# Finding the rows of each expert: one-hot tables for two experts, scattered records for six

## The reference

```python
logits = xf @ gate_w.T                      # xf: rotated rows, 4096 x 512; 8 experts
scores = softmax(logits); topv, topi = top_k(scores, 2)
gates = topv / sum(topv)
# loc: running number of a token at its expert, first choices of all tokens first
valid = loc < cap                            # cap = 1024
flat_idx = where(valid, topi * cap + loc, 0)
# per expert: h = relu(rows @ fc1.T + b1); eo = h @ fc2 + b2   (hidden width 2048)
out = x + sum_k eo[flat_idx_k] * gates_k * valid_k
```

## Time and profile before

| | us |
|---|---|
| median of three runs | 1426.5 |
| the profiled execution | 1426.91 |
| its span, first to last instruction | 1425.2 |
| TensorE busy in the span | 1370.5 |
| VectorE busy | 1062.8 |
| ScalarE busy | 702.3 |
| GpSimd busy | 303.1 |

### The profile page before, as it was taken

How to read it: one execution, slowest core, us unless ns; L and a number is a source line. 1 busy time by engine, 2 the same in 40 slices (tenths; PEclk the granted TensorE clock), 3 DMA queues, 4 the chain that set the end, 5 groups by cost and what they waited for, 6 DMA issues and landing times.

```text
span 1425.2 us, 17919 instructions
## 1 busy us (share of the span) xinstructions
PE 1370.5 (96%) x6109; PEld 1123.8 (79%) x6109; DVE 1062.8 (75%) x1610; ACT 702.3 (49%) x1050; POOL 303.1 (21%) x322
## 2 busy tenths in 40 slices
PE   8459999999999999999999999999999999999997
PEld 5347888888888888888888888888888888888885
DVE  6898879686886778686886878777796868855443
ACT  5336445555464455454465445554455454644442
POOL 1054302321024202231033201241032200220021
PEclk9759999999999999999999999999999999999999
DMA  8666575556466564575566564575555533543232
GB/s 296 230 164 143 119 157 146 174 121 148 83 197 157 115 129 129 145 163 132 97 176 167 105 139 108 163 168 135 98 169 145 112 79 61 161 119 68 51 105 71
DMA packets 448684, 194.15 MB, mean 136 GB/s; under 512 B 398432, under 2 KB 400617, under 8 KB 446674
## 3 DMA queue, kind: packets, MB, share of 16 engines
q1 hardware_dynamic: 426466, 125.98, 40.0%
q0 software_dynamic: 22128, 67.03, 14.9%
HBM read 153.21 MB, written 39.98 MB: 136 GB/s over the span
## 4 chain that ended last, share of the span: by engine, by line
PE 94%; DVE 3%; DMA 1%; issue 1%; ACT 0%; SPq 0%; POOL 0%; POOLq 0%; DVEq 0%
PE ps L1163 15%; PE ps L1155 15%; PE ps L1159 15%; PE ps L1130 14%; PE ps L1132 14%; PE ps L1131 14%; DVE yfull L902 1%; PE ps L1093 1%; PE ps L1146 1%; PE ps L1148 1%; PE ps L1147 1%; PE ps L1075 1%; DMA x_all<-in_x 1%; PE ps L1076 1%; DMA h<-in_x,gather_row 0%
## 5 line engine op out<-in xcount | busy, mean ns | idle before, releaser
L1130 PE MATMUL ps<-yc_hi,w1c_hi 128*128 128x512 f32 x896 | 350.5, 391 | 2.4 <-DVE yc_lo L868 1.2
L1132 PE MATMUL ps<-yc_hi,w1c_lo 128*128 128x512 f32 x896 | 349.4, 390 | 0.0
L1131 PE MATMUL ps<-yc_lo,w1c_hi 128*128 128x512 f32 x896 | 349.4, 390 | 0.0
L1155 PE MATMUL ps<-w_hi,h_hi 128*128 128x512 f32 x952 | 254.4, 389 | 0.0
L1163 PE MATMUL ps<-w_lo,h_hi 128*128 128x512 f32 x952 | 254.4, 389 | 0.0
L1159 PE MATMUL ps<-w_hi,h_lo 128*128 128x512 f32 x952 | 254.4, 389 | 0.0
L1163 PEld LDWEIGHTS ps<-w_lo,h_hi 128*128 128x128 f32 x952 | 178.7, 188 | 37.1
L1159 PEld LDWEIGHTS ps<-w_hi,h_lo 128*128 128x128 f32 x952 | 178.7, 188 | 37.1
L1155 PEld LDWEIGHTS ps<-w_hi,h_hi 128*128 128x128 f32 x952 | 178.7, 188 | 37.1
L1130 PEld LDWEIGHTS ps<-yc_hi,w1c_hi 128*128 128x128 f32 x896 | 168.7, 188 | 41.2 <-issue 3.3
L1132 PEld LDWEIGHTS ps<-yc_hi,w1c_lo 128*128 128x128 f32 x896 | 168.6, 188 | 35.4
(11 more groups left out here) (172 smaller groups left out, 1460.7 us busy)
## 6 DMA issues: line engine op xcount, KB each, us to landing
w_raw<-in_L_ffn_fc_w SPq DMA_DIRECT2D x232, 256.0 KB
w_raw<-in_L_ffn_fc_w SPq DMA_DIRECT2D x512, 64.0 KB
slots_dram<-x_blk POOLq DMA_DIRECT2D x28, 512.0 KB
x_blk<-slots_dram SPq DMA_DIRECT2D x224, 64.0 KB
out<-x_all SPq DMA_DIRECT2D x8, 1024.0 KB, 13.0
x_all<-in_x SPq DMA_DIRECT2D x7, 1024.0 KB, 13.7
b_bc<-in_L_ffn_fc_b POOLq DMA_DIRECT2D x8, 256.0 KB
x_all<-in_x SPq DMA_DIRECT2D x4, 256.0 KB, 3.7
```

The source lines that it names most:

```text
L1130: pe.matmul(bank, hi, yc_hi[:, y, q, :], start=first and q == 0, stop=False, skip_group_check=True)
L1131: pe.matmul(bank, hi, yc_lo[:, y, q, :], start=False, stop=False, skip_group_check=True)
L1132: ins = pe.matmul(bank, lo, yc_hi[:, y, q, :], start=False, stop=last and q == 1, skip_group_check=True)
L1155: pe.matmul(eo_s[:, b, :], h_hi[:, c, blk], w2_hi[:, w, :], start=False, stop=False, skip_group_check=True)
```

## The change

- `turn_logits` multiplies by a 16 x 8 matrix of ones at (e, e) and (e + 8, e), so that the sum of the two parts comes out of TensorE. The two choices are made on logits in PSUM, not on scores; the softmax needs the exponentials later only, with its subtraction and sums on GpSimd.
- The place of a token is worked out on VectorE for experts 0 and 1 alone. The slot order is new: slot s of an expert is block s mod 8, row s / 8. Tables are made for those two experts, one after the other (8 blocks wide, not 64), and their tokens are found by 2 x 32 matmuls. GpSimd gathers expert 0 after the first.
- GpSimd works out the slot of each of the 8192 (token, choice) pairs (`finish_records`) and scatters 64 times 128 records of 8 bytes (token + 1, gate) into a table in DRAM, then loads the table (`table_in`). VectorE reads it (`read_table`) at the end of group 6 of expert 0. The gathers of gates are gone. `store_x(V)` stands apart from `gather_x(V)`, with records between them.
- Expert 0: of the second 512 rows, ScalarE copies the turned rows to SBUF, VectorE rotates parts 2 and 3 (`rotate_half`, 6 instructions for 256 rows), and parts 0 and 1 come from 16 fp32 matmuls with identities scaled by the rotation (`diag`), in PSUM banks 4 and 5. `y_sum` reads them there, so `set_bits` on those banks waits for it. `keep_warm` has 1 matmul; `idle(3)` stands at seven places before.
- SyncE issues `cut_x(3)` after the weight loads of group 4, `cut_x(4)` after those of group 7, and `cut_x(5)` at tile 5 of fc2, for expert 0. For every expert, `load_b2` and the fourth `bring_x` come before `scatter_rows`.

The core of the diff:

```diff
+        diag = rows[:, 0:2, :].rearrange("p b (k n) -> p (b k) n", n=P)
+        x_upper = x_turned[:, :, :, :].rearrange("p b q n -> p (b q n)").rearrange("p (u j n) -> p u j n", u=2, j=Q)
...
         small_ps = wp_all[:, 0:9]
...
                     if G == 3:
                         cut_x(2)
+                    if G == 4:
+                        cut_x(3)
+                    if G == GROUPS - 1:
+                        cut_x(4)
...
+                    if e == 0 and tile == 5:
+                        cut_x(5)
...
+            pool.wait_ge(masked, 1)
+            pool.tensor_tensor(dl[:, :, :], score[:, :, :], mx.unsqueeze(2).to_broadcast([P, TJ, E]), ALU.subtract
+                               ).then_inc(shifted, 1)
...
+            link(pool.tensor_tensor(loc[:, :, :], cnt[:, :, :], ahead[:, :].unsqueeze(2).to_broadcast([P, TOPK * E, TJ]),
+                                    ALU.add))
+            link(pool.tensor_tensor(loc[:, :, :], loc[:, :, :], hot[:, :, :, :].rearrange("p k e j -> p (k e) j"), ALU.mult))
...
+            def finish_records():
+                by_e = loc[:, :, :].rearrange("p (k e) j -> p k e j", k=TOPK)
+                link(pool.tensor_tensor(loc_sums[:, :, 0:4, :], by_e[:, :, 0:4, :], by_e[:, :, 4:8, :], ALU.add))
+                link(pool.tensor_tensor(loc_sums[:, :, 4:6, :], loc_sums[:, :, 0:2, :], loc_sums[:, :, 2:4, :], ALU.add))
...
+                pool.wait_ge(scores_ready, 1)
+                for k in range(TOPK):
+                    ins = pool.tensor_tensor(rec_k[:, k, :], gate_parts[:, 3 + k, :], gate_parts[:, 5, :], ALU.mult)
+                ins.then_inc(records_ready, 1)
...
+            def scatter_records(columns):
+                for c in columns:
                     pool.indirect_dma_start(
-                        gates[:, at:at + 1], None, gates_dram,
-                        bass.IndirectOffsetOnAxis(ap=gate_row[:, at:at + 1], axis=0)).then_inc(gates_in, 16)
+                        table_dram, bass.IndirectOffsetOnAxis(ap=slot_row[:, c:c + 1], axis=0),
+                        records[:, c, :], None, bounds_check=E * CAP - 1, oob_is_err=False).then_inc(records_out, 16)
...
+            pool.wait_ge(slots_ready, 2)
             gather_x(0)
+            finish_records()
...
             load_b2(0)
             gather_x(1)
-            pool.wait_ge(gates_stored, 16)
-            gather_gates(0)
+            scatter_records(range(0, 4))
+            store_x(1)
+            scatter_records(range(4, 26))
+            pool.wait_ge(y12_done, 2)
             gather_rows(0)
+            gather_x(2)
+            scatter_records(range(26, 30))
+            store_x(2)
+            scatter_records(range(30, 46))
+            gather_x(3)
+            scatter_records(range(46, 50))
+            store_x(3)
+            scatter_records(range(50, TOPK * TJ))
+            pool.wait_ge(records_out, 16 * TOPK * TJ)
+            pool.dma_start(table[:, :, :].rearrange("p (e n) a -> p e (n a)", e=E),
+                           table_dram.rearrange("(e p n) a -> p e (n a)", e=E, n=NB)).then_inc(table_in, 16)
+            pool.wait_ge(tables_ready, 1)
...
-                scatter_rows(2 * e)
+                    bring_x(4 * e + 4)
+                    bring_x(4 * e + 5)
                 if not last:
                     load_b2(e + 1)
+                if e < E - 2:
+                    bring_x(4 * e + 6)
+                scatter_rows(2 * e)
...
+            w1_high_parts(0, 0)
+            w1_high_parts(0, 1)
...
+            for k in range(2 * Q):
+                ins = act.activation(diag[:, k, :], ident[:, :], ACT.Copy, scale=rot[:, k // Q, k % Q:k % Q + 1])
+            ins.then_inc(diag_ready, 1)
...
-            w1_high_parts(0, 0)
-            w1_high_parts(0, 1)
...
+                act.wait_ge(hot_t_ready, k + 1)
+                act.activation(hot_q[:, :, 1, :, :], hot_t[:, :, :, :], ACT.Copy, scale=part_f[:, :]).then_inc(hots_p_ready, 1)
...
+                if u < 2:
+                    first_term(xth[:, 4 * u, :], lambda i: yfull[:, i, u * UNIT:(u + 1) * UNIT])
+                else:
+                    act.activation(x_upper[:, u - 2, :, :].rearrange("p j n -> p (j n)"),
+                                   ps[:, 2 * u:2 * u + 2, :].rearrange("p b n -> p (b n)"), ACT.Copy).then_inc(x_kept, 1)
+                    act.wait_ge(x_kept, u - 1)
+                    first_term(x_upper[:, u - 2, 0, :], lambda i: yfull[:, i, u * UNIT:(u + 1) * UNIT], (2, 3))
...
-            link(dve.tensor_copy(lg_low[:, :, :], logits_hl[:, :, 1, :]))
-            link(dve.tensor_tensor(lg[:, :, :], logits_hl[:, :, 0, :], lg_low[:, :, :], ALU.add))
...
-            dve.tensor_tensor(dl[:, :, :], lg[:, :, :], per_e(mx), ALU.subtract).then_inc(shifted, 1)
-            dve.wait_ge(exps_ready, 1)
-            link(dve.reduce_sum(sm, ex[:, :, :], X))
-            link(dve.reciprocal(sm, sm))
-            link(dve.tensor_tensor(score[:, :, :], ex[:, :, :], per_e(sm), ALU.mult))
...
+                link(dve.reduce_max(v, from_, X))
+                link(dve.tensor_tensor(wt[:, :, :], from_, per_e(v), ALU.is_equal))
...
-                    link(dve.scalar_tensor_tensor(score[:, :, :], hot_k, -2.0, score[:, :, :], ALU.mult, ALU.add))
+                    dve.scalar_tensor_tensor(score[:, :, :], hot_k, -1e30, lg, ALU.mult, ALU.add).then_inc(masked, 1)
+                    dve.wait_ge(masked, 1)
...
-                dve.tensor_tensor(hot_t[:, c % 2, :, :, :], numbers[:, :, 0:BLOCKS, :], of_pairs(q_f[:, k, js], BLOCKS),
...
-                dve.tensor_tensor(hot_b[:, k, pairs, :, :], numbers, of_pairs(b_f[:, k, js], P), ALU.is_equal)
...
-                dve.tensor_tensor(hot_q[:, k, pairs, 0, :, :], hot_t[:, c % 2, :, :, :], of_pairs(j1[:, js], BLOCKS),
-                                  ALU.mult).then_inc(hots_ready, 1)
...
+            dve.tensor_copy(ahead[:, :], ahead_ps).then_inc(ahead_kept, 1)
+            link(first)
+            link(dve.tensor_tensor(loc01[:, :, :, :], loc01[:, :, :, :], hot[:, :, 0:2, :], ALU.mult))
+            link(dve.tensor_tensor(place01[:, :, :], loc01[:, 0, :, :], loc01[:, 1, :, :], ALU.add))
+            link(dve.scalar_tensor_tensor(place01[:, :, :], place01[:, :, :], float(CAP), place01[:, :, :], ALU.is_le, ALU.mult))
+            link(dve.tensor_scalar(place_i[:, :, :], place01[:, :, :], -1.0, None, ALU.add))
+            dve.tensor_scalar(n_i[:, :, :], place_i[:, :, :], NB - 1, None, ALU.bitwise_and)
+            link(dve.tensor_scalar(p_i[:, :, :], place_i[:, :, :], 3, None, ALU.arith_shift_right))
...
+            def block_table(k):
...
+                numbers = value[:, 0:NB, :].unsqueeze(1).to_broadcast([P, TJ // 2, NB, 2])
+                dve.tensor_tensor(hot_t[:, :, :, :], numbers, of_pairs(n_f[:, k, :], TJ // 2, NB), ALU.is_equal).then_inc(hot_t_ready, 1)
+                dve.wait_ge(hot_t_ready, k + 1)
+                dve.tensor_tensor(hot_q[:, :, 0, :, :], hot_t[:, :, :, :], of_pairs(j1[:, :], TJ // 2, NB), ALU.mult)
...
+            def row_table(k, part, parts):
...
+                numbers = value[:, :, :].unsqueeze(1).to_broadcast([P, m, P, 2])
+                dve.tensor_tensor(hot_b[:, pairs, :, :], numbers, of_pairs(p_f[:, k, 2 * part * m:2 * (part + 1) * m], m, P),
+                                  ALU.is_equal).then_inc(hots_ready, 1)
...
+            def make_scores():
...
+                link(dve.reciprocal(s1, sm))
+                link(dve.tensor_tensor(s2_, e2, s1, ALU.mult))
+                link(dve.tensor_tensor(both, s1, s2_, ALU.add))
+                dve.reciprocal(both, both).then_inc(scores_ready, 1)
...
+            def read_slots(k):
...
+                dve.wait_ge(hots_used, k + 1)
+                link(dve.tensor_reduce(token1[:, rows_k], token_ps[k].rearrange("p a n -> p n a"), X, ALU.add))
+                dve.tensor_scalar(gather_row[:, rows_k], token1[:, rows_k], -1.0, 0.0, ALU.add, ALU.max).then_inc(slots_ready, 1)
+            block_table(0)
+            for part in range(4):
+                row_table(0, part, 4)
+            block_table(1)
+            row_table(1, 0, 2)
+            read_slots(0)
+            row_table(1, 1, 2)
             w1_low_parts(0, 1)
-            dve.wait_ge(hots_used, 2 * TOPK)
-            link(dve.tensor_copy(j_part[:, :], token_ps[:, 0, :]))
-            link(dve.scalar_tensor_tensor(token1[:, :], token_ps[:, 1, :], float(TJ), j_part[:, :], ALU.mult, ALU.add))
-            dve.tensor_scalar(gather_row[:, :], token1[:, :], -1.0, 0.0, ALU.add, ALU.max).then_inc(slots_ready, 1)
...
-                    dve.tensor_tensor(t1, y12, y11, ALU.subtract).then_inc(yt_done, 1)
+                    if e == 0:
+                        dve.wait_ge(y12_done, 2)
+                    dve.tensor_tensor(t1, y12 if e else ps[:, 4:6, :], y11, ALU.subtract).then_inc(yt_done, 1)
...
-                    dve.tensor_tensor(y12, y22, y12, ALU.subtract).then_inc(yt_done, 1)
```

(53 more changed lines are left out.)

289 lines of the change are left out of this document (145 added, 144 removed).

## The result

The changed kernel takes 1438.64 us (1436.97 to 1441.1, 6 runs) against 1426.72 (1424.32 to 1427.61): ratio 1.0088, 95% interval 1.0077 to 1.0099. It is 12 us slower, where 1416.8 was forecast. Its profiled execution takes 1439.7, with a span of 1437.7, 12.5 over that of before.

The account below looks back on a forecast made before the run. TensorE was taken to bound the kernel from 114 us on, a chain of single engines before. From 1426.9, 12.6 gained at the start and 2.9 lost to records gave 1417.2, median 1416.8; own range 1413 to 1421.

Parts of the forecast that it names:

- Bound, and gain ahead of 114 us: TensorE bounds from 114 us on; the gain lies in the earlier chain of single engines, steady flow 12.6 us earlier.
- Logits, +2.6: turn_logits on TensorE: its added fp32 multiplications are paid in full, +2.6 us (bounds 0 and 5.4).
- Choices, places, GpSimd's arithmetic: Start, before the first table: choices on logits -3.6 us, places of two experts -1.9, GpSimd arithmetic beside VectorE +1.2.
- rival 4: VectorE waits for GpSimd's arithmetic throughout, 7.5 us in place of 1.2: 1423.5, median 1423.1; chance 0.12.
- D: The time at which the first token table stands, forecast at 60.0 us.
- Rotation, -5.0: VectorE's rotation for expert 0: 48 instructions become 24 + 12, -5.0 us; y_sum(0) at 90.2 against 103.26.
- Added wait: TensorE waits for y_sum(2) before set_bits; preceding idle time may bring half clock: +0.5 us (0 to 2).
- rival 3: Fillers don't keep the clock; 16 diag matmuls at half clock take 13.8 us: 1421.9, median 1421.5; chance 0.08.
- Records, +2.9: GpSimd's record scatters at 1.34 us each put store_x(3) at 167.2, its block 2.9 us late for S4.
- rival 2: Record scatters slower: from 1.53 us each the whole gain is gone; at 1.63, 1431.7, median 1431.3; chance 0.13.
- Table "nothing", `turn_x(4)` "0 (at most 1)": Table in SBUF by 196, read_table asks about 202: no cost; turn_x(4) some 3 late, costing 0 (at most 1).
- Rival 1: SyncE's order, not GpSimd, times turn_x(3): say 1.2 us late, 1415.1; chance 0.27.

Follow-up runs that it names:

- x3_later: Changed kernel with 28 record scatters instead of 20 between store_x(2) and store_x(3), 8 fewer behind it; 1448.32 us, ratio 1.0162.
- after_again: The changed kernel as it is, run again on chip C; median 1440.41 us, ratio 1.0091.
- x3_ahead: Changed kernel with 4 record scatters instead of 20 between store_x(2) and store_x(3), the 16 others after store_x(3); 1425.51 us, ratio 0.9998.
- cut3_early: x3_ahead with SyncE issuing cut_x(3) straight behind cut_x(2), after the loads of group 3 instead of group 4; 1423.72 us, ratio 0.9987.
- turns_transposed: turn4_late with the logits turned by transposes of both halves and added on VectorE, instead of fp32 matmuls; 1414.67 us, ratio 0.9928 (chip A).
- turn4_late: cut3_early with turn_x(4) on VectorE behind the fourth item of expert 0's second phase, not the first; 1418.82 us, ratio 0.9953.
- records_nowhere: turns_transposed with every record's row set beyond the table's end: 64 scatters issued, no element written; median 1463.43 us on chip C.
- turns_transposed_third: turns_transposed unchanged, run on chip C as control for records_nowhere and another run; median 1455.56 us.

## Why the prediction was wrong

The sum, 1417.2, against the 1439.7 of the profiled execution, in us: `store_x(3)` 15.2 late; 0.8 more from it to S4; 1.5 for the slow clock behind the stall (13.9 from S4's first matmul to the next `keep_c22`, for 12.4 before); 6.1 for the second stall; 1.3 back later; 0.3 outside the span. 15.2 + 0.8 + 1.5 + 6.1 - 1.3 + 0.3 = 22.6, where 22.5 is to be explained.

- *Bound, and gain ahead of 114 us*: right in the place, not in the size. The start gains 6.7 in the profiled execution for the 12.6 forecast, below the 8 that the prediction itself named as a sign of being wrong. The place of the loss was right: "the time lost after the start" is at `turn_x(3)` first, and at `turn_x(4)`.
- *Logits, +2.6*: mis-sized. The first maximum stands at 48.8 to 51.2 in the eight traces with fp32 turns (mean 50.3) and at 44.8 to 47.9 in the eleven with transposes (mean 46.3), which do the two additions (0.92) ahead of it: 4.0 + 0.9 = 4.9, near the upper bound of 5.4. I priced a fp32 multiplication by its two loads at full clock, 0.16, which is the least that my own rows allowed. The 64 matmuls of line 1205 are recorded at 0.251 each, two for a multiplication.
- *Choices, places, GpSimd's arithmetic*: from the first operation on the logits to the scan it is 5.6 (51.00 to 56.62) for 9.1 before (45.87 to 54.98), -3.5 for -3.6. The arithmetic held VectorE's two operations for 0.95 + 1.31 - 0.46 = 1.8 where 1.2 was taken; rival 4's 7.5 did not come, since an operation on `loc` takes 1.06 to 1.26, not 3.0. By the Trainium skill (SBUF — State Buffer, Who interferes with whom) the two engines take turns at a shared port; the trace agrees for these two, each of which ends 0.1 behind the GpSimd operation beside it. With the turns, D was 63.1 for 60.0.
- *Tables to gather 5.6, to rotation 12.9*: 5.9 and 13.3, right.
- *Rotation, -5.0*: right in the instructions, and the 16 products with `diag` took 7.15, 0.45 each, as forecast. But the second unit waited 2.44 for ScalarE in the profiled execution, which had itself waited 4.97 for TensorE's turns of the gathered rows; `y_sum(0)` came at 96.56 for 90.2. In x3_later, whose start is the same code, it came at 91.71: the start varies by 5 between executions, which one profile doesn't show. "12.6 earlier" was 6.7 here, 11.6 in x3_later.
- *Added wait, rival 3*: the clock was 1.00 from 82 us on, so rival 3, which priced the half clock at `diag` (86 to 93), is wrong. Nor did the added wait, 2.80 here, lower it. But the fillers did not bring the clock up at once: it was 0.50 up to 80. That is at most a part of the 2.44 above, since after_again has the same wait (2.52) with the clock at 1.00 from 78 on.
- *Records, +2.9*: the step that failed. The structure of this term was right, down to the wait on `x_blk`; the price was not. 1.34 was taken from scatters of rows, which take 0.98 to 1.39 in the trace before. Here the records took 1.54 in front of `store_x(3)` (91.50 to 182.37 is 90.9; less eight gathers 12.2 and two stores 1.6, 77.1 for 50), as the early gate gathers of the earlier trace rows had warned with 1.63. 50 x 0.20 = 10.1, 3.8 from the later start and 1.3 from gathers and stores make 182.4 of 167.2. TensorE stood 12.76 where 2.9 was reckoned. This is rival 2, which had 0.13 and said that the whole gain is gone from 1.53 on; but its own sum, 1417.2 + 10 at this price, falls 12.5 short as well, for the later start, the slow clock and `turn_x(4)` above all.
- *Clock behind a stall*: left out of the sum. The clock is 0.50 during the 12.76 of idle time and 0.86 in the 10 us behind it; the stall cost 14.4, and the second, 3.93 long, 6.1.
- *Table "nothing", `turn_x(4)` "0 (at most 1)"*: wrong. The table load was issued at 204.37 and took about 2.9, for "in SBUF by 196"; the first stall hides that in the kernel after, and in four of the kernels where it is gone VectorE waits 2.5 to 3.9 for the table. For `turn_x(4)` I counted the table's arrival and not what starts only with `read_table`: three DMAs and a queue behind it, 23 us, while `turn_x(4)` asked for its end 16 after its start. It costs 6.1 in the kernel after, 4.8 in the runs. "The fc2 tiles are two ahead" was no cover: `h_lo`, which TensorE needs for the next tile, stands behind `turn_x(4)` on VectorE.
- *Rival 1*: in part. With GpSimd out of the way, SyncE's order leaves 4.7 of waiting before `turn_x(3)` (x3_ahead), with 0.55 of TensorE standing; taking that wait away (cut3_early) brought 1.6, within the noise.

## What to carry to other kernels

Price a stream of DMAs on GpSimd by the row that has the same neighbours (here 1.27 + 0.30 beside a busy VectorE, 1.28 in all alone), not by the same kind of instruction elsewhere, and multiply before choosing: 50 times 0.2 was 10 of the 22 us that were missed. A result that is "in time" opens a chain that starts only when it is read; count that chain up to its last consumer, and what is queued behind the waiter. And put work that others wait for ahead of bulk work in an in-order queue: that order alone was worth 12.8 us here.

## What the runs showed of the hardware

- With a stream of some 60 indirect DMAs on GpSimd, ScalarE and VectorE waited up to 28 us for releases that come from no operation on record, on two chips of those used and not in every kernel there. The kernel before, whose DMAs of this kind come in bursts of eight, took 1425 to 1427 on all (medians).
- A TensorE idle for 2.38 at the head of turns_transposed was followed by matmuls of 512 columns at 0.63 instead of 0.39, half clock, for some 3 us. One of 1.63 in turn4_late was not, and neither was the longer one of 2.80 at the same place of the kernel after: the length of the idle time alone doesn't decide it. The two lines, of turns_transposed and of the kernel after, with four matmuls in 2.04 and in 1.16:

```profile
91.83 2.04 PE L1335 MATMUL ps<-yc_hi,w1c_hi 128*128 128x512 f32 x4 [2.38 <-DVE yfull L955]
```

```profile
100.32 1.16 PE L1333 MATMUL ps<-yc_hi,w1c_hi 128*128 128x512 f32 x4 [2.80 <-DVE yfull L953]
```

- By the Trainium skill (DMA: Bandwidth & Descriptors, Specifications) transfers below 512 bytes are read-modify-write. In records_nowhere nothing is written and GpSimd is busy about as long (70.70 of 100 for 73.95 in turns_transposed_third): what GpSimd spends is the issue, not the write. Whether a write of 8 bytes is a read-modify-write no run here shows.
